# Nine-step Newton roots, layer-norm roots in the heads' chain, and three more tiles turned early

## The chip, the cores and the metric

The kernel runs on one core of one Trainium2 chip. The metric is the time of one execution on the device in microseconds (us). The time to compare with is the median of several runs of the same kernel; one further execution is taken with the hardware profiler, and all rows below are from that one.

## The reference, cut to what matters

The input x is 4 x 512 rows of 512 values. Two layers are added to it.

```
x = x + attn(layernorm(x))            # 16 heads of 32, linear attention with decay, chunks of 128
    q, k = rotate(silu(xn @ Wq)), rotate(silu(xn @ Wk));  v = xn @ Wv
    per chunk: scores = (q k^T) * D;  o = scores v + (q * decay_q) S;  S = lam S + (k * decay_k)^T v
    o = rmsnorm_per_head(o * sigmoid(xn @ Wg1 @ Wg2)) * norm_weight;  return o @ Wo
x = x + ffn(layernorm(x))             # weights in 4-bit codes with a scale per 32
    gelu(x @ Wg^T) * (x @ Wu^T) @ Wd^T      with MLP_DIM = 4096
```

Both the layer norm (one root for each row of x) and the norm of the gated heads (16 roots for each row) need a reciprocal square root.

## The kernel before, in words

Everything is written out by hand: each engine has its own program, in order, and the engines meet at semaphores. There is no scheduler; the order of the lines of an engine's program is the order of its work.

**Attention.** The 2048 rows are 16 tiles of 128 (`t = 4 * b + c`, batch b, chunk c). Tiles 0 to 13 are the body `tile(b, c)` of each engine, 14 and 15 are written out in `passage()`, interleaved with the first products and transposes of the second layer (`x1`, `x1_sums`, `gate`, `up`). In one tile TensorE does in order: `qk_transpose(t)` (line 1256, from `qr`); `k_project(t+1)` (12 matmuls); `gate1(t+1)`; `v_project(t+1)` (12); the scores (line 1341); `x_transpose(t+2)`; `o_part(t-1)` (12, the output projection of the tile before); `inter` (not in chunk 0) and `intra`; the state product (not in chunk 3); `q_part(t+2)` (12) with `o_back(t)` (line 1381) in its midst; `gate2(t+1)`. Products of 32-bit data are three matmuls of high and low parts (lines 1242 to 1244).

`o_transpose(t-1)` (line 1256, from `sq`) stands before `v_project` where t is in `TURNED_EARLY`, and after it elsewhere. Where t is in `TURNED_EARLY`, `gate1(t+1)` is also done `together`: four matmuls over 256 columns (line 1307), high and low parts side by side, which VectorE then adds (`sum_gate`); elsewhere it is eight over 128 columns (lines 1303, 1304). In tile 14 `o_transpose` stands before `v_project` too.

**VectorE** (DVE) does in one tile: `normed(t-1)`: wait for ScalarE's square, a sum per head (line 733), the root of 16 values a row by Newton's method (`newton`, lines 651 to 658, eleven steps, each waiting for the one before), and the multiplication that makes `sq` (line 737); `decayed_q(t)` (`qdT`, line 839); gate, rotation (`rope_of`, line 803) and low parts in an order that depends on `TURNED_EARLY`; `masked(t)`, four operations on the scores (line 845); `add_x1(t-1)` with the statistics of the finished row; then, in some tiles, more; then `gated(t)` (line 727), which needs `o_back(t)`; and the state. What "more" is: `stats_r(8, 16, 3)` in tile 4 and `stats2(0)`, `stats2(1)` in tiles 11 and 13 are the layer norm's roots, with a Newton chain of their own; `unit_bits` in tiles 5, 7, 9 (five operations, lines 760 to 771, which unpack 4-bit codes in `stg`) and `unit_scale` in tiles 6, 8, 10 (line 777).

After `gated(t)` ScalarE (ACT) squares `xg`, and `normed(t)` of the next tile can go on. GpSimd (POOL) does the second half of the rotation (lines 1096, 1104), the decayed keys, the sums and low parts of the unpacked weights, and from tile 12 on `x1_sums(n)`, eight groups for the second layer, each four scalings and four sums.

**Second layer.** 32 `pair`s in a loop (`blocks`), 14 products a pair and the rows of the pair before, with VectorE and ScalarE in their shade.

Of the kernel before, what the change touches and what calls it, by code (L numbers as in the profile page):

```python
# [52 lines left out]
TURNED_EARLY = (2, 3, 4, 6, 7, 9, 11, 12)  # L53
# [28 lines left out]
def build(nc, x, wq, wk, wv, wo, wg1, wg2, norm_w, packed, scales,  # L82
          rot, mask, decay_q, decay_k, lam_c, ident, out):
    ctx = ExitStack()
    with ctx:
# [20 lines left out]
        nt_v = sb("nt_v", [P, 16])  # L106
        nt_t = sb("nt_t", [P, 16])
# [11 lines left out]
        with ExitStack() as att:  # L119
# [30 lines left out]
            rr = sb("rr", [P, HEADS], F32, att)  # L150
# [74 lines left out]
        st_scaled, st_done = sem("st_scaled"), sem("st_done")  # L225
        xg_done, sq_done, ms_done, on_done = (sem("xg_done"), sem("sq_done"), sem("ms_done"),
# [16 lines left out]
        NT = 11  # L243
# [394 lines left out]
        def _(dve):  # L638
            V = nc.vector

            def newton(steps, v, n, r, base, scale, eps):

                vv, tt = nt_v[:, 0:n], nt_t[:, 0:n]
# [7 lines left out]
                done(V.tensor_scalar(vv, v, scale, eps, ALU.mult, ALU.add))  # L651
# [78 lines left out]
            def normed(t):  # L730
# [5 lines left out]
                newton(s_nt, ms[:], HEADS, rr[:], NT * t, 1.0 / HD, 4 * RMS_EPS)  # L736
                V.tensor_tensor(sq[:].rearrange("p (h d) -> p h d", d=HD),
                                xg[:].rearrange("p (h d) -> p h d", d=HD),
                                rr[:].unsqueeze(2).broadcast_to([P, HEADS, HD]),
# [16 lines left out]
            def unit_bits(k):  # L756
# [13 lines left out]
                dve.wait_ge(dq_bits, k5 + 4)  # L770
# [12 lines left out]
            def stats2(n):  # L783
# [7 lines left out]
                newton(s_ntl, ln2[:, rows, 1], last - first, r2[:, rows], NT * (4 + n), 1.0,  # L791
# [231 lines left out]
            def pair(q, p):  # L1023
# [19 lines left out]
                if p == 1 and ready:  # L1043
                    unit_bits(UNITS + GATE)
# [721 lines left out]
```

## Time and profile before

| what | value |
|---|---|
| median of 3 runs | 1284.52 us (1284.4 to 1286.33) |
| the profiled execution, its own time | 1285.71 us |
| its span, first to last instruction | 1283.5 us |
| TensorE busy | 1268.5 us, 99% |
| VectorE busy | 915.4 us, 71% |
| ScalarE, GpSimd busy | 476.7 us, 439.7 us |
| mean granted clock of TensorE | 0.999 |

In the rows below a time is in microseconds from the span's start. PE is TensorE, DVE VectorE, ACT ScalarE, POOL GpSimd. Matmuls are pipelined: the duration of one reaches into the next, so the cost of a matmul is read from one start to the next. The idle time in brackets is the engine's time without work before that row, and behind the arrow stands what ended it. The attention stage lasts to about 315 us, with the passage from about 273 to 340; the rest is the loop.

### The profile page before, as it was taken

The page shows a single profiled execution, that of the slowest core. Times are in us where ns is not written, and L with a number is a line of the kernel's source. Part 1 is how long each engine was busy: PE and PEld are TensorE (multiplying, and loading weights), DVE is VectorE, ACT ScalarE, POOL GpSimd, SP SyncE. Part 2 cuts the span into 40 slices and gives each one's busy share as a digit, 9 for nine tenths or more (in the row PEclk, how much of TensorE's full clock was granted, in tenths as well). Part 3 has the DMA queues.
Part 4 walks back from the last instruction along what each step waited for, and adds up shares of the span by engine and source line. Part 5 has one row for each costly group of instructions (what it writes and reads, how often), then busy time and mean ns, then how long its engine had stood idle before and what let it go on. Part 6 is the DMA issues. An engine that isn't in the chain of part 4 may idle for free.

```text
span 1283.5 us, 20667 instructions
## 1 busy us (share of the span) xinstructions
PE 1268.5 (99%) x7344; PEld 1042.4 (81%) x7344; DVE 915.4 (71%) x1602; ACT 476.7 (37%) x807; POOL 439.7 (34%) x360
## 2 busy tenths in 40 slices
PE   9999999999999999999999999999999999999998
PEld 6888877887788888888888888888888888888887
DVE  7888788788867667676667676766767676767565
ACT  5433443434433333333333333333333333333321
POOL 2434553674432232324132423233232324232400
PEclk9999999999999999999999999999999999999999
DMA  9000000000001011000000000100001010000003
GB/s 324 13 1 3 17 17 2 2 1 2 28 22 33 16 33 32 17 33 32 25 25 25 25 31 18 33 16 33 25 25 33 25 33 25 25 25 25 25 14 118
DMA packets 21778, 40.23 MB, mean 31 GB/s; under 512 B 2660, under 2 KB 2916, under 8 KB 21604
## 3 DMA queue, kind: packets, MB, share of 16 engines
q1 hardware_dynamic: 21060, 39.47, 9.5%
q8 instruction: 31, 0.51, 0.2%
q10 hardware_dynamic: 672, 0.13, 0.1%
q14 instruction: 15, 0.12, 0.0%
HBM read 35.40 MB, written 4.19 MB: 31 GB/s over the span
## 4 chain that ended last, share of the span: by engine, by line
PE 90%; DVE 6%; POOL 1%; issue 1%; ACT 0%; DVEq 0%; POOLq 0%
PE bank L1401 15%; PE bank L1403 15%; PE bank L1404 15%; PE bank L1242 12%; PE bank L1244 12%; PE bank L1243 12%; PE bank L1256 2%; PE bank L1341 1%; PE bank L1360 1%; DVE pr L845 1%; PE bank L1393 1%; PE bank L1350 1%; DVE nt_t L657 1%; PE bank L1381 0%; POOL ws L1178 0%
## 5 line engine op out<-in xcount | busy, mean ns | idle before, releaser
L926 DVE TENSOR_TENSOR acc<-acc,bank 128x512 f32<-128x512 f32 x248 | 169.6, 684 | 134.8 <-PE bank L1244 134.8
L1243 PE MATMUL bank<-wdl,hh 128*128 128x512 f32 x512 | 199.2, 389 | 0.0
L1242 PE MATMUL bank<-wdh,hh 128*128 128x512 f32 x512 | 199.2, 389 | 0.0
L1244 PE MATMUL bank<-wdh,hl 128*128 128x512 f32 x512 | 199.2, 389 | 0.0
L1401 PE MATMUL bank<-xoh,wuh 128*128 128x512 f32 x448 | 175.1, 391 | 0.7 <-ACT cxa L506 0.7
L1401 PE MATMUL bank<-xoh,wgh 128*128 128x512 f32 x448 | 175.1, 391 | 0.6 <-DVE cxa L934 0.6
L1404 PE MATMUL bank<-xoh,wul 128*128 128x512 f32 x448 | 174.4, 389 | 0.0
L1404 PE MATMUL bank<-xoh,wgl 128*128 128x512 f32 x448 | 174.3, 389 | 0.0
L1403 PE MATMUL bank<-xol,wuh 128*128 128x512 f32 x448 | 174.3, 389 | 0.0
L1403 PE MATMUL bank<-xol,wgh 128*128 128x512 f32 x448 | 174.3, 389 | 0.0
L1150 POOL TENSOR_TENSOR wdl<-ws,wdh 128x512 fp32r<-128x512 f32 x32 | 48.5, 1539 | 307.5 <-ACT wdh L432 307.5
L942 DVE TENSOR_TENSOR hl<-hx,hh 128x512 fp32r<-128x512 f32 x128 | 104.8, 819 | 51.4 <-ACT hh L513 51.1
L513 ACT ACTIVATE hh<-hx 128x512 fp32r<-128x512 f32 x128 | 80.6, 631 | 157.1 <-DVE hx L938 156.9
L506 ACT ACTIVATE cxa<-bank 128x512 f32<-128x512 f32 x64 | 38.3, 598 | 215.9 <-PE bank L1404 215.9
L1242 PEld LDWEIGHTS bank<-wdh,hh 128*128 128x128 f32 x512 | 96.1, 188 | 20.0
L1244 PEld LDWEIGHTS bank<-wdh,hl 128*128 128x128 f32 x512 | 96.1, 188 | 20.0
L1243 PEld LDWEIGHTS bank<-wdl,hh 128*128 128x128 f32 x512 | 96.1, 188 | 19.9
L1143 POOL TENSOR_TENSOR wul<-ws,wuh 128x896 fp32r<-128x896 f32 x32 | 74.2, 2339 | 84.6 <-ACT wuh L428 84.6
L1401 PEld LDWEIGHTS bank<-xoh,wuh 128*128 128x128 f32 x448 | 84.1, 188 | 18.6 <-ACT cxa L506 1.4
L1401 PEld LDWEIGHTS bank<-xoh,wgh 128*128 128x128 f32 x448 | 84.1, 188 | 18.6 <-DVE cxa L934 1.0
L1404 PEld LDWEIGHTS bank<-xoh,wgl 128*128 128x128 f32 x448 | 84.1, 188 | 17.5
L1404 PEld LDWEIGHTS bank<-xoh,wul 128*128 128x128 f32 x448 | 84.1, 188 | 17.5
(170 smaller groups left out, 2280.9 us busy)
## 6 DMA issues: line engine op xcount, KB each, us to landing
stg<-packed_dram SPq DMA_DIRECT2D x48, 256.0 KB, 2.6
stg<-scales_dram SPq DMA_DIRECT2D x48, 256.0 KB
out_dram<-acc SPq DMA_DIRECT2D x16, 256.0 KB, 2.1
acc<-x_dram SPq DMA_DIRECT2D x3, 1024.0 KB, 14.8
w_in<-wq_dram SPq DMA_DIRECT2D x2, 512.0 KB, 5.3
w_in<-wk_dram SPq DMA_DIRECT2D x2, 512.0 KB, 7.2
w_in<-wv_dram SPq DMA_DIRECT2D x2, 512.0 KB, 8.9
w_in<-wo_dram SPq DMA_DIRECT2D x2, 512.0 KB, 11.5
```

The costliest lines, as they stand in the source:

```text
L506: A(dst, src[:], ACT.Copy).then_inc(signal, 1)
L513: A(hh[n][:], hx[n][:], ACT.Copy).then_inc(h_hi[n], 1)
L926: V.tensor_tensor(row, row, BY[j % 2][:], ALU.add).then_inc(y_add, 1)
L942: V.tensor_tensor(hl[n][:], hx[n][:], hh[n][:].bitcast(F32), ALU.subtract).then_inc(h_lo[n], 1)
L1143: nc.gpsimd.tensor_tensor(lo[:, piece, :, :], ws[:, piece, :, :], hi[:, piece, :, :].bitcast(F32), ALU.subtract).then_inc(dq_lo, 1)
L1150: nc.gpsimd.tensor_tensor(wdl[:, piece, :].rearrange("p (s m) -> p s m", s=4), ws[:, piece, 0:4, :], wdh[:, piece, :].bitcast(F32) .rearra ...
L1242: pe.matmul(dst, w_h, x_h, start=start, stop=False)
L1243: pe.matmul(dst, w_h, x_l, start=False, stop=False)
L1244: return pe.matmul(dst, w_l, x_h, start=False, stop=stop)
L1401: pe.matmul(dst[:], w_h, x_h, start=start and a == 0, stop=False, skip_group_check=True)
L1403: pe.matmul(dst[:], w_h, x_l, start=False, stop=False, skip_group_check=True)
L1404: ins = pe.matmul(dst[:], w_l, x_h, start=False, stop=a == 1, skip_group_check=True)
```

## The change

It has these parts.

- `TURNED_EARLY` has 5, 8 and 10 in addition.
- `newton` takes nine steps in place of eleven, for all its callers: two refinements of another form in place of three.
- The layer norm's roots of rows 8 to 15 (tile 4), of the second norm's rows 0 to 7 (tile 11) and 8 to 12 (tile 13) are no longer made in those tiles. `normed_and_rows` makes them in tiles 5, 12 and 14, in the chain that makes the heads' roots there: the aggregates and `var_of` before, up to 24 values in the chain, `roots_out` after.
- The bits of units 1 and 2 (tiles 7 and 9) and the scaling of them (tiles 8 and 10) stand right after `normed(t-1)`; the last of the five operations of `unit_bits` is now `unit_join`, and is done right before the scaling there.
- GpSimd's `x1_sums(2)` stands first in `passage()`, ahead of the last tile's rotation.
- In `pair`, `low_of(C22, ...)` stands ahead of the first `total`.

```diff
-TURNED_EARLY = (2, 3, 4, 6, 7, 9, 11, 12)
+TURNED_EARLY = (2, 3, 4, 5, 6, 7, 8, 9, 10, 11, 12)
...
-        NT = 11
+        NT = 9
...
-                for _ in range(3):
-                    done(V.scalar_tensor_tensor(out=tt, in0=r, scalar=-0.5, in1=r,
-                                                op0=ALU.mult, op1=ALU.mult))
-                    done(V.tensor_tensor(tt, tt, vv, ALU.mult))
-                    done(V.scalar_tensor_tensor(out=r, in0=tt, scalar=1.5, in1=r,
-                                                op0=ALU.add, op1=ALU.mult))
+                done(V.tensor_tensor(tt, r, r, ALU.mult))
+                done(V.tensor_tensor(tt, tt, vv, ALU.mult))
+                done(V.scalar_tensor_tensor(out=tt, in0=tt, scalar=-10.0 / 3.0, in1=tt,
+                                            op0=ALU.add, op1=ALU.mult))
+                done(V.scalar_tensor_tensor(out=r, in0=tt, scalar=5.0, in1=r,
+                                            op0=ALU.add, op1=ALU.mult))
+                done(V.scalar_tensor_tensor(out=tt, in0=r, scalar=-27.0 / 1024.0, in1=r,
+                                            op0=ALU.mult, op1=ALU.mult))
+                done(V.tensor_tensor(tt, tt, vv, ALU.mult))
+                done(V.scalar_tensor_tensor(out=r, in0=tt, scalar=9.0 / 16.0, in1=r,
+                                            op0=ALU.add, op1=ALU.mult))
...
+            def var_of(ln, first, last):
+
+                V.tensor_scalar(nt_v[:, HEADS:HEADS + last - first], ln[:, first:last, 1], 1.0,
+                                LN_EPS, ALU.mult, ALU.add).then_inc(var_in, 1)
+
+            def roots_out(ln, r, nm, first, last, k, signal, n):
+                rows, new = slice(first, last), rr[:, HEADS:HEADS + last - first]
+                V.scalar_tensor_tensor(out=nm[:, rows], in0=ln[:, rows, 0], scalar=-1.0, in1=new,
+                                       op0=ALU.mult, op1=ALU.mult).then_inc(nm_out, 1)
+                dve.wait_ge(nm_out, k + 1)
+                V.tensor_copy(r[:, rows], new).then_inc(signal, n)
+
+            def normed_and_rows(t, ln, r, nm, first, last, k, signal, n):
+                for row in range(first, last):
+                    if signal is s_r1:
+                        dve.wait_ge(s_bn1, row + 1)
+                        V.bn_aggr(ln[:, row, :], bst1[:, row, :]).then_inc(s_ln1, 1)
+                    else:
+                        dve.wait_ge(bst_done, row + 1)
+                        V.bn_aggr(ln[:, row, :], bst1[:, row, :]).then_inc(ln2_done, 1)
+                dve.wait_ge(s_ln1 if signal is s_r1 else ln2_done, last)
+                var_of(ln, first, last)
+                dve.wait_ge(var_in, k + 1)
+                normed(t, last - first)
+                roots_out(ln, r, nm, first, last, k, signal, n)
...
-                dve.wait_ge(dq_bits, k5 + 4)
+
+            def unit_join(k):
+                dve.wait_ge(dq_bits, 5 * k + 4)
                 V.tensor_tensor(nib, nib, pk, ALU.bitwise_or).then_inc(dq_bits, 1)
...
-                if not at_start(b, c):
+                if t == 5:
+                    normed_and_rows(4, ln1, r1, nm1, 8, 16, 0, s_r1, 2)
+                elif t == 12:
+                    normed_and_rows(11, ln2, r2, nm2, 0, 8, 1, s_r2, 1)
+                elif not at_start(b, c):
                     normed(t - 1)
+                if t in UNIT_BITS[1:]:
+                    unit_bits(UNIT_BITS.index(t))
+                if t in UNIT_SCALE[1:]:
+                    unit_join(UNIT_SCALE.index(t))
+                    unit_scale(UNIT_SCALE.index(t))
                 decayed_q(t)
...
-                if t == 4:
-                    stats_r(8, 16, 3)
-                if t == 11:
-                    stats2(0)
-                if t == 13:
-                    stats2(1)
-                if t in UNIT_BITS:
-                    unit_bits(UNIT_BITS.index(t))
-                if t in UNIT_SCALE:
-                    unit_scale(UNIT_SCALE.index(t))
+                if t == UNIT_BITS[GATE]:
+                    unit_bits(GATE)
+                    unit_join(GATE)
+                if t == UNIT_SCALE[GATE]:
+                    unit_scale(GATE)
                 gated(t)
...
-                normed(s - 1)
+                normed_and_rows(s - 1, ln2, r2, nm2, 8, 13, 2, s_r2, 1)
...
+                low_of(C22, P_ - 1)
                 dve.wait_ge(g_ps, 7 * P_ + 2)
                 dve.wait_ge(g_copy, 3 * P_ + 1)
                 total(GB[:], GB, hx[C11][:], g_sum)
-                low_of(C22, P_ - 1)
                 up_12(P_ - 1)
...
             def passage():
+                x1_sums(2)
                 rope_b_(TILES - 1, CHUNKS - 1)
                 scaled(BATCH - 1, CHUNKS - 2)
-                for n in range(2, 8):
+                for n in range(3, 8):
                     x1_sums(n)
```

## Rows read from the trace of the kernel before

**Rows 1.** The page, busy time of each engine

```profile
PE 1268.5 (99%) x7344; PEld 1042.4 (81%) x7344; DVE 915.4 (71%) x1602; ACT 476.7 (37%) x807; POOL 439.7 (34%) x360
```

**Rows 2.** TensorE's timeline, the first instructions of tiles 4 to 11: start, duration

```profile
92.99 1.03 PE L1256 MATMUL bank<-idt,qr 128*128 128x128 f32 x8
...
109.68 1.04 PE L1256 MATMUL bank<-idt,qr 128*128 128x128 f32 x8
...
127.92 1.03 PE L1256 MATMUL bank<-idt,qr 128*128 128x128 f32 x8
...
145.72 1.04 PE L1256 MATMUL bank<-idt,qr 128*128 128x128 f32 x8
...
163.13 1.04 PE L1256 MATMUL bank<-idt,qr 128*128 128x128 f32 x8
...
182.26 1.03 PE L1256 MATMUL bank<-idt,qr 128*128 128x128 f32 x8
...
199.95 1.03 PE L1256 MATMUL bank<-idt,qr 128*128 128x128 f32 x8
...
220.38 1.03 PE L1256 MATMUL bank<-idt,qr 128*128 128x128 f32 x8
```

**Rows 3.** TensorE's timeline, the gate's first part in tile 7 and tile 8

```profile
149.35 0.64 PE L1307 MATMUL bank<-xt,g1s 128*128 128x256 f32 x4
149.82 0.60 PE L1256 MATMUL bank<-idt,sq 128*128 128x128 f32 x4
...
166.76 0.22 PE L1303 MATMUL bank<-xt,g1s 128*128 128x128 f32 x1
...
167.60 0.45 PE L1242 MATMUL bank<-w_hi,xt 128*128 128x512 f32 x1
```

**Rows 4.** VectorE's timeline, from the gated product of tile 6 to `sq`

```profile
143.60 0.69 DVE L727 SCALAR_TENSOR_TENSOR xg<-tg,bank 128x512 f32<-128x512 f32 x1 [1.04 <-PE bank L1381]
...
145.71 0.18 DVE L651 TENSOR_SCALAR nt_v<-ms 128x16 f32<-128x16 f32 x1
...
148.01 0.69 DVE L737 TENSOR_TENSOR sq<-xg,rr 128x512 f32<-128x512 f32 x1
```

**Rows 5.** TensorE's timeline, `o_back` of tile 7

```profile
161.07 0.60 PE L1381 MATMUL bank<-idt,xg 128*128 128x128 f32 x4
```

**Rows 6.** VectorE's timeline, from the gated product of tile 7 to `sq`

```profile
164.31 0.68 DVE L727 SCALAR_TENSOR_TENSOR xg<-tg,bank 128x512 f32<-128x512 f32 x1
...
168.30 1.20 DVE L657 TENSOR_TENSOR nt_t<-nt_t,nt_v 128x16 f32<-128x16 f32 x1
...
170.78 0.69 DVE L737 TENSOR_TENSOR sq<-xg,rr 128x512 f32<-128x512 f32 x1
```

**Rows 7.** VectorE's groups by line: busy us, mean ns, idle before

```profile
L777 DVE SCALAR_TENSOR_TENSOR ws<-stg 128x1024 f32<-128x1024 f16 x48 | 58.5, 1219 | 0.0
...
L763 DVE SCALAR_TENSOR_TENSOR stg<-stg 128x512 int32<-128x512 int32 x48 | 35.8, 745 | 1.6
```

**Rows 8.** TensorE's timeline, idle before `sq`'s transposes in tile 12 and the passage

```profile
242.50 0.66 PE L1256 MATMUL bank<-idt,sq 128*128 128x128 f32 x4 [0.46 <-DVE sq L737]
...
278.82 0.66 PE L1256 MATMUL bank<-idt,sq 128*128 128x128 f32 x4 [0.84 <-DVE sq L737]
...
294.46 0.65 PE L1256 MATMUL bank<-idt,sq 128*128 128x128 f32 x4 [1.15 <-DVE sq L737]
```

**Rows 9.** VectorE's timeline, the Newton chain in tile 13

```profile
255.14 0.17 DVE L651 TENSOR_SCALAR nt_v<-ms 128x16 f32<-128x16 f32 x1
...
259.25 0.69 DVE L737 TENSOR_TENSOR sq<-xg,rr 128x512 f32<-128x512 f32 x1
```

**Rows 10.** ScalarE's timeline at the start of the kernel

```profile
8.60 0.81 ACT L359 ACTIVATE xn<-acc,nm,r 128x512 f32<-128x512 f32 x1 [1.20 <-DVE nm L675]
```

**Rows 11.** GpSimd's timeline, its rotation for tile 15

```profile
278.33 2.85 POOL L1096 TENSOR_TENSOR rb<-qa,rotT 128x512 f32<-128x512 f32 x2 [2.01 <-ACT qa L397]
```

**Rows 12.** Windows: busy us and instructions by engine, granted clock, DMA share, GB/s

```profile
298.00:300.00 2.00, 2.00 (x11) 2.00 (x10) 0.64 (x2) 1.38 (x4) 0.23 (x1) 0.50 0.00 0
```

More of the change, by code:

```diff
@@ L105, in build @@
         nm2 = sb("nm2", [P, TILES])
-        nt_v = sb("nt_v", [P, 16])
-        nt_t = sb("nt_t", [P, 16])
+        nt_v = sb("nt_v", [P, 24])
+        nt_t = sb("nt_t", [P, 24])
         bst1 = sb("bst1", [P, TILES, 6])
@@ L639, in _, with newton @@
             V = nc.vector
-            def newton(steps, v, n, r, base, scale, eps):
-                vv, tt = nt_v[:, 0:n], nt_t[:, 0:n]
+            def newton(steps, v, n, r, base, scale, eps, more=0):
+                vv, tt = nt_v[:, 0:n + more], nt_t[:, 0:n + more]
                 k = [0]
@@ L649, in done @@
                     dve.wait_ge(steps, base + k[0])
-                done(V.tensor_scalar(vv, v, scale, eps, ALU.mult, ALU.add))
+                done(V.tensor_scalar(nt_v[:, 0:n], v, scale, eps, ALU.mult, ALU.add))
                 done(V.tensor_scalar(r.bitcast(I32), vv.bitcast(I32), -0.5, RSQRT_SEED,
                                      ALU.mult, ALU.add))
-                for _ in range(3):
-                    done(V.scalar_tensor_tensor(out=tt, in0=r, scalar=-0.5, in1=r,
-                                                op0=ALU.mult, op1=ALU.mult))
-                    done(V.tensor_tensor(tt, tt, vv, ALU.mult))
-                    done(V.scalar_tensor_tensor(out=r, in0=tt, scalar=1.5, in1=r,
-                                                op0=ALU.add, op1=ALU.mult))
+                done(V.tensor_tensor(tt, r, r, ALU.mult))
[9 more added lines that the diff above has]
+                                            op0=ALU.add, op1=ALU.mult))
                 assert k[0] == NT
@@ L728, in gated, with normed @@
                                        op0=ALU.add, op1=ALU.mult).then_inc(xg_done, 1)
-            def normed(t):
+            def var_of(ln, first, last):
[20 more added lines that the diff above has]
+                roots_out(ln, r, nm, first, last, k, signal, n)
+            def normed(t, more=0):
                 dve.wait_ge(sq_done, t + 1)
@@ L735, in normed @@
                 dve.wait_ge(ms_done, t + 1)
-                newton(s_nt, ms[:], HEADS, rr[:], NT * t, 1.0 / HD, 4 * RMS_EPS)
+                newton(s_nt, ms[:], HEADS, rr[:, 0:HEADS + more], NT * t, 1.0 / HD, 4 * RMS_EPS, more)
                 V.tensor_tensor(sq[:].rearrange("p (h d) -> p h d", d=HD),
                                 xg[:].rearrange("p (h d) -> p h d", d=HD),
-                                rr[:].unsqueeze(2).broadcast_to([P, HEADS, HD]),
+                                rr[:, 0:HEADS].unsqueeze(2).broadcast_to([P, HEADS, HD]),
                                 ALU.mult).then_inc(on_done, 1)
@@ L790, in stats2 @@
                 dve.wait_ge(ln2_done, last)
-                newton(s_ntl, ln2[:, rows, 1], last - first, r2[:, rows], NT * (4 + n), 1.0,
+                newton(s_ntl, ln2[:, rows, 1], last - first, r2[:, rows], NT * (1 + n), 1.0,
                        LN_EPS)
@@ L1044, in pair @@
                     unit_bits(UNITS + GATE)
+                    unit_join(UNITS + GATE)
                 if p == 1 and not last:
@@ L1056, in pair @@
                     unit_bits(3 * q + DOWN)
+                    unit_join(3 * q + DOWN)
                 y(4)
@@ L1068, in pair @@
                     unit_bits(3 * q + 3 + UP)
+                    unit_join(3 * q + 3 + UP)
                 y(6)
@@ L1071, in pair @@
                     unit_bits(3 * q + 3 + GATE)
+                    unit_join(3 * q + 3 + GATE)
                 if p == 1 and not last:
```

3 lines of the change are left out of this document (2 added, 1 removed).

## The prediction

> **What bounds the kernel now.** I read the page first: TensorE is busy for 99% of the span [rows 1], so only two things can save time, fewer TensorE microseconds or fewer gaps between them. The second view is TensorE's own timeline in the attention stage. A tile begins with the eight transposes of the rotated q and k (line 1256, out of `qr`). From one such row to the next is a tile's length [rows 2]: tile 4 takes 109.68 - 92.99 = 16.69 us, tile 5 18.24, tile 6 17.80, tile 7 17.41, tile 8 19.13, tile 9 17.69 and tile 10 20.43. Tiles 4, 6, 7 and 9 are turned early, tiles 5, 8 and 10 are not. A tile's work depends on its chunk: chunk 0 has no `inter`, chunk 3 no state product. So tile 8 (chunk 0) is to be compared with tile 4, tile 5 (chunk 1) with tile 9, and tile 10 (chunk 2) with tile 6. The third view is VectorE's timeline, for what TensorE waits for at `o_transpose`: the normed heads `sq`.
>
> VectorE's clean chain is that of tile 6 into 7 [rows 4]: the gated product starts at 143.60, as soon as `o_back` is there, and the multiplication that ends `normed` at 148.01, so 4.41 us plus about 0.7 for the multiplication, 5.1 in all. Eleven Newton steps fill 145.71 to 148.01, 0.21 us each. Early TensorE comes to `o_transpose` at 149.82, which is 4.10 after the tile's start at 145.72 [rows 2, 3], and finds `sq` done since 148.7. Tile 7 into 8 is the unclean chain. `o_back` starts at 161.07 and takes 0.6 [rows 5], yet the gated product starts only at 164.31, because `unit_bits(1)` stands ahead of it in VectorE's queue, and then two Newton steps show 1.20 us or so in place of 0.17 [rows 6], in which GpSimd holds what they need. The multiplication starts at 170.78 and TensorE has long run dry. Tile 10 repeats this with `unit_bits(2)`.
>
> **The change, part by part.**
>
> *Turned early, 5, 8 and 10.* The first part of the gate takes four matmuls of 256 columns in place of eight of 128: 149.82 - 149.35 = 0.47 us against 167.60 - 166.76 = 0.84 [rows 3]. That is 0.37 a tile. The trace's 128-column matmuls therefore cost 0.105 apiece and the 256-column ones 0.118. The Trainium skill (TensorE: Matmul & The Clock Gate, Back-to-back issue gap) makes the gap proportional to columns above an issue floor, about 56 ns at 128 and twice that at 256. By it the merging would save nothing and the sum below would be 1.1 us smaller; the trace disagrees, with 0.84 against 0.47, and I go by the trace. The rest of what an early tile saves is smoother order, and is in the tile lengths. Tile 5 has no long wait now, so it goes from 18.24 to tile 9's 17.69: **0.55 us**.
>
> *Tiles 8 and 10.* Early order asks for `sq` at 4.10 after the tile's start, 167.23 in tile 8's present times, though it is done only at 171.5 now. What makes it earlier: `unit_bits` of tiles 7 and 9 moves ahead of `decayed_q`, so the gated product starts at 161.07 + 0.63 = 161.70, not 164.31 (2.6 us); the chain falls 2.6 earlier, before GpSimd's rotation starts on q, so the two long steps become short (2.05 us); and there are nine steps in place of eleven (0.42). 161.70 + 5.1 - 0.42 = 166.4, with 0.8 to spare. So the tiles should reach the clean lengths: tile 8 19.13 - 16.69 = **2.44 us**, tile 10 20.43 - 17.80 = **2.63 us**. Bounds: nothing gained at all, when the chain is late by 2.5 and more, and those two numbers.
>
> *What the moved work meets.* Ahead of `decayed_q`, tiles 8 and 10 now have the join and the scaling, about 0.7 and 1.22 us [rows 7], and tiles 7 and 9 the bits, some 2.1 us by the 0.745 of the costliest of four [rows 7]. TensorE needs `qdT` and the gate's sum before the scores, 7.4 us after the start. 3.3 (end of `sq`) + 1.9 + 0.7 + 0.3 = 6.2, covered by 1.2 us. Masking then starts perhaps 0.3 late, since the rotation on VectorE may have to let GpSimd finish; after it TensorE still has the scores, the transposes of x and `o_part`, so this costs nothing. Without that cover each of the four tiles would lose up to 1.9 us. The rule behind it is that of the Trainium skill (SBUF — State Buffer, SBUF: two separate sides): VectorE operations with two SBUF inputs and GpSimd's exclude each other for a whole instruction. The 1.20 us steps [rows 6] agree with it, and it would forbid moving two-input work into GpSimd's time; the join, the rotation and the Newton steps are such work.
>
> *The shared chains.* In tile 4 `stats_r(8,16)` delays the gated product, in tile 11 `stats2(0)` and in tile 13 `stats2(1)`. Now rows join the chain of the heads: what stays of each are the aggregates (some 0.6 for eight), one scaling before, a product and a copy after, 0.2 each. Aggregates and scaling lie beside ScalarE's square, which VectorE waits for anyway (0.5), and push the chain by 0.2 to 0.5; the product and the copy come after `sq`. TensorE's stalls at those places are 0.46 idle in tile 12 and 0.84 in tile 14 [rows 8], to which the pipeline's drain adds about 0.15 (in tile 8 0.94 idle is 1.09 from start to start). In tile 12 I take all of it, **0.6**. In tile 14 the chain will meet GpSimd's second x group as that of tile 13 meets the first: there eleven steps took 255.14 to 259.25, 4.11 in place of 2.3 [rows 9]. By that row `sq` ends 4.5 after the start, with TensorE there at 4.46. I take **0.7** of 1.0, between 0 and 1.0.
>
> *Two steps fewer elsewhere.* At the start of the kernel ScalarE waits 1.20 us for VectorE's first root [rows 10] and TensorE's first projection hangs on it: two steps of 0.2, **0.4 us** (0 if a load or ScalarE's casts come last). At 294.46 TensorE sits idle for 1.15 behind `sq` of tile 14 [rows 8]; two steps and about 0.4 of slowing by GpSimd, whose third group no longer lies there, give **0.8** (0.4 to 1.3). For the last two groups of rows, the end of the transposes and the first pair, where VectorE is again last, I allow **0.4** (0 to 1.2).
>
> *GpSimd's third group* goes into its idle 2.01 us ahead of the rotation for tile 15 at 278.33 [rows 11], and is longer than that (the four x scalings and four sums), so that rotation comes some microseconds later; TensorE transposes what it makes only after the stall at 294.46 [rows 8], 14 us on. Cost 0.
>
> *The pair loop.* `low_of(C22)` goes ahead of the first total. TensorE shows no gap in the loop's 30 pairs that VectorE could close or open: 0. The joins there only follow their bits: 0.
>
> **Sum.** 0.55 + 2.44 + 2.63 + 0.6 + 0.7 + 0.4 + 0.8 + 0.4 = 8.5 us. The profiled execution took 1285.71 (span 1283.5), which would be 1277.2; it lies 1.2 above the median of the runs, 1284.52, and against that, which is what the new time is compared with, the forecast is 1276.0.
>
> **Rivals.**
>
> 1. *The clock stays up.* Between 298 and 300 the granted clock is 0.50 [rows 12], 1.2 GHz, after the gap ahead of 294.46 [rows 8]. Where the clock is at 0.50 matmul work takes twice as long, so 3 us at it cost 1.5. Shorter gaps there may keep it at 2.4 GHz and give that back: 1274.5. Against it: by my own count some of the gap remains. The Trainium skill (TensorE: Matmul & The Clock Gate, The HAM clock gate) says that recent activity keeps the gate open, which allows this but doesn't decide it.
>
> 2. *GpSimd still holds the chain.* In tiles 8 and 10 two steps are lengthened as now, 2.05 us [rows 6]: `sq` ends 5.3 after the start, not 3.3, TensorE waits 1.2 in each, and 0.5 is lost behind tile 5, whose bits still stand ahead of the gated product: 1276.0 + 2.9 = 1278.9. For it: GpSimd's sums after a scaling now start at another time. Against it: its rotation waits for ScalarE's q, which comes after the chain.
>
> 3. *The other side: early order asks for what is still late.* If the gated product of tiles 7 and 9 is not freed, `sq` of tile 8 ends at 171.5, and early TensorE stands from 167.2: 4.2 of waiting in place of the 2.44 and 2.63 lost now. With the bits' and the scaling's 1.9 us each before `qdT` on top, which have no cover then, that is 1.8 + 1.6 + 3.8 = 7.2 more than now, less the other 3.4: 1288.3. It decides against the change from about 5.5 us of lateness in each of the two tiles on. Against it: `o_back` is done 2.6 before the gated product starts [rows 5, 6], and nothing but the bits lies between.
>
> 4. *The gaps only move.* What tiles 8 and 10 gain is given back where VectorE is nearly full, in tiles 9, 11 and the passage, because everything comes earlier for TensorE but not for VectorE: within 0.2% of 1284.5.
>
> **How the numbers follow.** Forecast 0.66, the clock 0.12, GpSimd 0.14, gaps that move 0.05, the other side 0.03. A difference of 0.2%, 2.6 us, is about what can be told from no change. Faster are the first three, 0.92; same 0.05; slower 0.03. The range goes from the clock's case with all bounds good, 1273.2, to the GpSimd case with its smaller terms lost, 1280.6.
>
> **What would show it.** Tile lengths near 17.7 for tile 5, 16.7 for 8 and 17.8 for 10; the gated product 0.6 after `o_back` starts in tiles 7, 9, 11 and 13; no idle of TensorE before the transposes of `sq` in tiles 8, 10 and 12; nine steps in each chain; GpSimd's third group ahead of the last rotation. The prediction is wrong if the transposes of `sq` in tiles 8 and 10 have idle time of more than a microsecond ahead of them, if scores wait for `qdT`, or if the passage between 273 and 340 grows.

## The result, and the profile after

The changed kernel takes 1277.34 us in the median of 4 runs (1275.86 to 1278.02), the kernel before in the same set 1284.91 (1284.4 to 1286.33). The ratio is 0.994, with a 95% interval of 0.9925 to 0.9954: faster by 0.5 to 0.75%. The forecast was 1276.0. In a second set of 5 runs the same changed kernel took 1276.63, ratio 0.9938 (0.9925 to 0.9952), against 1284.50 for the kernel before in that set. The profiled execution has a span of 1276.0 (before 1283.5); its own time is 1278.02, the longest of its set.

The head of the page after, to be read against [rows 1]:

```profile
span 1276.0 us, 20589 instructions
PE 1264.7 (99%) x7332; PEld 1040.4 (82%) x7332; DVE 897.2 (70%) x1535; ACT 479.1 (38%) x810; POOL 439.9 (34%) x360
```

VectorE has 18 us less to do. TensorE is busy for 3.8 us less and idle for 3.7 less (15.0 before, 11.3 after), so the gain lies half in its work and half in its gaps. TensorE's timeline, the first transposes of each tile from 4 to 13, against [rows 2]:

```profile
92.34 1.03 PE L1299 MATMUL bank<-idt,qr 128*128 128x128 f32 x8
109.02 1.04 PE L1299 MATMUL bank<-idt,qr 128*128 128x128 f32 x8
126.73 1.04 PE L1299 MATMUL bank<-idt,qr 128*128 128x128 f32 x8
144.44 1.04 PE L1299 MATMUL bank<-idt,qr 128*128 128x128 f32 x8
161.85 1.03 PE L1299 MATMUL bank<-idt,qr 128*128 128x128 f32 x8
178.54 1.03 PE L1299 MATMUL bank<-idt,qr 128*128 128x128 f32 x8
196.24 1.04 PE L1299 MATMUL bank<-idt,qr 128*128 128x128 f32 x8
213.95 1.03 PE L1299 MATMUL bank<-idt,qr 128*128 128x128 f32 x8
231.36 1.03 PE L1299 MATMUL bank<-idt,qr 128*128 128x128 f32 x8
248.05 1.04 PE L1299 MATMUL bank<-idt,qr 128*128 128x128 f32 x8
```

From start to start: tile 4 16.68, tile 5 17.71, tile 6 17.71, tile 8 16.69, tile 10 17.71, tile 12 16.69. From tile 4 to 12 every tile of one chunk number now has one length. Tile 13 (chunk 1), which is not turned early, takes 18.21 as tile 5 did before. In tile 8 the gate's product takes 0.47 from start to start, as [rows 3] had it for an early tile, and the transposes of `sq` have no idle time ahead of them:

```profile
165.46 0.63 PE L1350 MATMUL bank<-xt,g1s 128*128 128x256 f32 x4
165.93 0.60 PE L1299 MATMUL bank<-idt,sq 128*128 128x128 f32 x4
```

VectorE's timeline from tile 7 into 8, against [rows 4, 6]:

```profile
160.43 0.69 DVE L733 SCALAR_TENSOR_TENSOR xg<-tg,bank 128x512 f32<-128x512 f32 x1 [2.15 <-PE bank L1424]
161.81 0.69 DVE L765 TENSOR_REDUCE ms<-sq 128x16 f32<-128x512 f32 x1 [0.70 <-ACT sq L419]
162.53 0.17 DVE L652 TENSOR_SCALAR nt_v<-ms 128x16 f32<-128x16 f32 x1
...
164.21 0.18 DVE L664 SCALAR_TENSOR_TENSOR rr<-nt_t,rr 128x16 f32<-128x16 f32 x1
164.42 0.69 DVE L769 TENSOR_TENSOR sq<-xg,rr 128x512 f32<-128x512 f32 x1
165.03 0.68 DVE L805 TENSOR_TENSOR stg<-stg 128x512 int32<-128x512 int32 x1
165.75 1.22 DVE L811 SCALAR_TENSOR_TENSOR ws<-stg 128x1024 f32<-128x1024 f16 x1
166.89 0.68 DVE L873 TENSOR_TENSOR qdT<-bank,dqT 128x512 f32<-128x512 f32 x1
```

VectorE now idles 2.15 us in wait of `o_back` where it was late before, the nine steps are 0.21 apart, and `sq` is done at 165.1, 0.8 before TensorE asks for it. The join and the scaling stand behind it, as planned, and `qdT` is there 1.6 before the scores, which start at 169.22.

The idle places of the passage, TensorE's timeline, against [rows 8]; the last one, at 320.96, has its counterpart in one of 0.24 at 328.02 in the kernel before:

```profile
271.18 0.66 PE L1299 MATMUL bank<-idt,sq 128*128 128x128 f32 x4 [0.30 <-DVE sq L769]
286.29 0.66 PE L1299 MATMUL bank<-idt,sq 128*128 128x128 f32 x4 [0.60 <-DVE sq L769]
...
320.96 0.41 PE L1436 MATMUL bank<-idt,ws 128*128 128x128 f32 x2 [1.17 <-POOL stg L1228]
```

And the stretches of the passage in which the clock fell, against [rows 12] (engines' busy time, then the granted clock, the DMA share and GB/s):

```profile
288.00:290.00 2.00, 1.37 (x7) 1.40 (x8) 2.00 (x6) 0.98 (x3) 1.92 (x4) 0.65 0.02 4
290.00:292.00 2.00, 2.00 (x11) 2.00 (x10) 0.47 (x1) 1.38 (x4) 0.62 (x1) 0.50 0.00 0
```

The granted clock was 0.50 (1.2 GHz) for 3.4 us, from 288.6 to 292.0, as it was from 297.0 to 300.4 in the kernel before. So none of the 7.5 us is the clock's.

**Where the time came from.** The lead of after over before, read at the same instruction in both traces: 0.44 at the first tiles, 7.09 at tile 14's start, 8.17 at the transposes of `sq` at 286.29, 8.02 at the first product of the second layer (298.76), 7.06 at 320.96, 7.55 at the last pair, 7.5 at the end. So 8.2 were gained by 286, which is more than the kernel has at the end: about 1 us is lost again in one place, between 298.76 and 320.96.

What is late there is VectorE. Its timeline, the last row's root chain of the kernel before and of the one after:

```profile
324.01 0.17 DVE L789 BATCH_NORM_AGGREGATE ln<-bst 128x2 f32<-128x6 f32 x1
324.59 0.28 DVE L655 SCALAR_TENSOR_TENSOR nt_t<-r 128x1 f32<-128x1 f32 x1
...
327.19 0.69 DVE L870 TENSOR_TENSOR xol<-bank,xoh 128x512 fp32r<-128x512 f32 x1
```

```profile
316.00 0.17 DVE L823 BATCH_NORM_AGGREGATE ln<-bst 128x2 f32<-128x6 f32 x1
316.59 0.42 DVE L655 TENSOR_TENSOR nt_t<-r 128x1 f32<-128x1 f32 x1
...
317.62 0.57 DVE L659 SCALAR_TENSOR_TENSOR r<-nt_t,r 128x1 f32<-128x1 f32 x1
...
319.56 0.65 DVE L827 SCALAR_TENSOR_TENSOR nm<-ln,r 128x1 f32<-128x1 f32 x1
320.13 0.68 DVE L904 TENSOR_TENSOR xol<-bank,xoh 128x512 fp32r<-128x512 f32 x1
```

With eleven steps it took 3.18 us from the aggregate to the next low part; with nine it takes 4.13. The low part `xol` frees the bank that TensorE's transposes at 320.96 write; the row's label names GpSimd's `stg`, but these transposes read `ws`, whose last sum had ended at 316.44; that `stg` belongs to the next group. GpSimd works beside the chain all the time, on the seventh group of sums:

```profile
316.42 2.27 POOL L1220 TENSOR_SCALAR stg<-acc,r,nm 128x256 f32<-128x256 f32 x4
```

### The profile page after: what moved, and what is told of

Its sections match the earlier page's. It is cut to its first block, busy times and chain, and to the rows that moved or that the text cites. A ratio compares the mean times of both kernels' runs of the same rounds, so it can differ in the third digit from the quotient of the medians.

```text
span 1276.0 us, 20589 instructions
## 1 busy us (share of the span) xinstructions
PE 1264.7 (99%) x7332; PEld 1040.4 (82%) x7332; DVE 897.2 (70%) x1535; ACT 479.1 (38%) x810; POOL 439.9 (34%) x360
## 4 chain that ended last, share of the span: by engine, by line
PE 94%; DVE 2%; POOL 1%; issue 0%; ACT 0%; POOLq 0%; DVEq 0%
PE bank L1444 16%; PE bank L1446 16%; PE bank L1447 15%; PE bank L1285 13%; PE bank L1287 13%; PE bank L1286 13%; PE bank L1299 2%; PE bank L1384 1%; PE bank L1403 1%; PE bank L1393 1%; PE bank L1436 1%; PE bank L1424 1%; DVE xol L904 0%; PE bank L1350 0%; PE bank L1416 0%
## 5 line engine op out<-in xcount | busy, mean ns | idle before, releaser
L980 DVE TENSOR_TENSOR hl<-hx,hh 128x512 fp32r<-128x512 f32 x128 | 101.7, 795 | 52.1 <-ACT hh L514 51.6
```

What stands on the lines that cost most here:

```text
L980: V.tensor_tensor(hl[n][:], hx[n][:], hh[n][:].bitcast(F32), ALU.subtract).then_inc(h_lo[n], 1)
```

## The experiments

Twelve runs follow: eleven edits and the changed kernel once more. They ran in three sets, in which the kernel before took 1284.71 (`a`, `b`, `c`, `e`), 1285.54 (`d`, `f`, `g`, `h`) and 1284.50 (`after_again`, `j`, `m`, `n`); between sets the ratios are to be compared, not the medians. "Lengths" are tile lengths as above. "The passage" is split at three rows that every trace has: tile 14's start, the first product of the second layer (the gate's), and the gate's product of the first pair that waits for `cxa` (343.92 in after). In the tables, "chain" is from the last row's aggregate to VectorE's next operation on 128 x 512.

### Early order, the moved units, the shared chains

`a_no_early`: the early list as before, all else changed. `b_early_only`: the kernel before with the new list alone. `c_units_late`: the units' bits, join and scaling back ahead of `gated`. `e_own_chains`: the layer norm's rows in chains of their own.

```diff
 a:  TURNED_EARLY = (2, 3, 4, 6, 7, 9, 11, 12)          # in the changed kernel
 b:  TURNED_EARLY = (2, 3, 4, 5, 6, 7, 8, 9, 10, 11, 12) # in the kernel before
 c: -if t in UNIT_BITS[1:]: ...   -if t in UNIT_SCALE[1:]: ...
    +if t in UNIT_BITS: unit_bits(...); unit_join(...)     # ahead of gated(t)
    +if t in UNIT_SCALE: unit_scale(...)
 e: -normed_and_rows(...)  in tiles 5, 12, 14
    +normed(t - 1);  stats_r(8, 16, 3), stats2(0), stats2(1) in tiles 4, 11, 13
```

> The changed kernel with the old list of tiles turned early (5, 8 and 10 not). Theory one, the freed chain: nearly all of the gain is that VectorE delivers sq in time, and the early order is worth some 0.5 us a tile; tiles 5, 8 and 10 become 18.2, 17.2 and 18.2 us, TensorE has no wait for sq there, and the time is 1277.3 + 1.5 = 1278.8. Theory two, the order: the gain comes with the early order and goes with it; tiles 8 and 10 go back to about 19.1 and 20.4, and the time is about 1282.9.

> The kernel before with 5, 8 and 10 turned early and nothing else. The freed chain: in tiles 8 and 10 TensorE comes to the transposes of sq 4.2 us before sq is there; tiles of some 20.9 and 22 us, tile 5 between 17.7 and 18.3, in all 2 to 3.5 us slower than before, about 1287.6. The order: tiles 5, 8 and 10 near 17.7, 16.7 and 17.8, about 1279.3.

> The changed kernel with the bits and scalings of units 1 and 2 back at the end of their tiles, ahead of the gated product. The freed chain: sq of tiles 7 and 9 is late again by 2.6 us and meets GpSimd's rotation, TensorE waits 3 to 4 us before its transposes in tiles 8 and 10, 7 us in all: 1284.3. The order, or the shorter chains, being the cause: no change, 1277.3.

> The changed kernel with the layer norm's roots back in chains of their own at the end of tiles 4, 11 and 13. If the shared chain is what freed tiles 5, 12 and 14: waits of TensorE for sq of about 0.6, 0.3 and 0.8 us there, 1.4 us slower than the changed kernel, 1278.7. If nine steps and the rest do it without the sharing: no such waits, 1277.3.

| kernel | median, ratio (95%) | span | tile 5 | tile 8 | tile 10 | tile 12 |
|---|---|---|---|---|---|---|
| before | 1284.91 | 1283.5 | 18.24 | 19.13 | 20.43 | 17.38 |
| after | 1277.34, 0.994 (0.9925, 0.9954) | 1276.0 | 17.71 | 16.69 | 17.71 | 16.69 |
| a_no_early | 1277.81, 0.9944 (0.9928, 0.9961) | 1275.8 | 18.20 | 17.14 | 18.22 | 16.68 |
| b_early_only | 1294.78, 1.0084 (1.0067, 1.0101) | 1291.1 | 18.80 | 22.56 | 23.88 | 17.37 |
| c_units_late | 1283.4, 0.9995 (0.9985, 1.0004) | 1280.2 | 17.71 | 19.55 | 20.84 | 16.69 |
| e_own_chains | 1277.66, 0.9948 (0.9932, 0.9965) | 1275.6 | 17.98 | 16.69 | 17.70 | 16.67 |

`a_no_early` gave the lengths of its first theory. The early order alone makes the kernel slower, by 10 us in the medians and by 7.6 in the span of the profiled executions, of which 7.4 lie in tiles 5, 8 and 10; I had expected 2 to 3.5. With the other parts it is worth 0.49 + 0.45 + 0.51 = 1.45 us by the lengths; the ratios of after and `a_no_early`, 0.994 and 0.9944, don't tell the two apart. TensorE's timeline of `b_early_only` shows what it asks for too early:

```profile
172.03 1.12 PE L1256 MATMUL bank<-idt,sq 128*128 128x128 f32 x4 [4.10 <-DVE sq L737]
212.52 0.71 PE L1256 MATMUL bank<-idt,sq 128*128 128x128 f32 x4 [4.37 <-DVE sq L737]
```

That is rival 3's 4.2, in the kernel where its condition holds. What I had left out is the clock: behind each of the two waits it fell to 1.2 GHz for 3.4 us, which costs half of that (windows, columns as above).

```profile
172.00:174.00 2.00, 1.98 (x7) 1.79 (x8) 0.96 (x3) 0.80 (x2) 0.00 (x0) 0.51 0.03 8
213.00:215.00 2.00, 2.00 (x7) 1.62 (x6) 1.36 (x4) 1.21 (x3) 0.00 (x0) 0.50 0.04 8
```

The clean length, the wait and 1.7 for the clock make up the tiles: 16.7 + 4.1 + 1.7 = 22.5 for tile 8 (22.56), 17.8 + 4.4 + 1.7 = 23.9 for tile 10 (23.88). With the chains shortened but the units left in place, in `c_units_late`, there is still 2.7 and 2.9 of waiting at the same two places:

```profile
168.98 0.66 PE L1294 MATMUL bank<-idt,sq 128*128 128x128 f32 x4 [2.67 <-DVE sq L769]
206.50 0.66 PE L1294 MATMUL bank<-idt,sq 128*128 128x128 f32 x4 [2.93 <-DVE sq L769]
```

So the move of two small groups of VectorE instructions carries 2.86 + 3.13 = 6.0 us under the early order, and with the units in their old place the kernel is no faster than before (0.9995). In the profiled execution of `c_units_late` the clock did not fall in these tiles; four of its ten runs took 1285.0 to 1286.6 at a mean clock of 0.996 or 0.997, the other six 1282.3 to 1283.4 at 0.999 or 1.0. Without the early order it and the shorter chain still give 1.99 + 2.21 (`a_no_early` against before). The parts don't add up one by one: early order is minus 7.4 without the move, about 3.4 of it the clock's, and plus 1.45 with it.

The shared chains are worth less than I had them. In `e_own_chains` tile 12 is as short as in after, and so it is in `d_eleven_steps` below (16.67), which shares the chain and keeps eleven steps: either part alone gives the 0.69. What taking the sharing away costs is 0.27 in tile 5 and 0.56 in tile 14, where the idle time before `sq` is 0.85 instead of 0.30. That makes 0.8 us by the trace; the ratios (0.9948 and 0.994) don't tell it from nothing.

### The nine steps

`d_eleven_steps`: the changed kernel with three Newton steps, eleven instructions, as in before.

```diff
-NT = 9     +NT = 11
-two refinements, seven steps     +for _ in range(3): ... three steps each
```

> The changed kernel with the root chain of eleven steps (three Newton steps) of before in place of the nine. By the sum: the chains in tiles 5 to 13 are off the path that sets the end, so their tiles keep their lengths (16.7 to 17.7); 0.4 comes back at the start (39.0 to 39.4), 0.3 to 0.4 in tile 14 or at the idle of 0.60 before scores(15), 0.3 at x1(23): together about 1.0, 1278.3 (1277.9 to 1278.8). A rival, that the chains still set the gate in tiles 8 and 10: 0.4 more for each, 1279.1 or above. Another, that the one row's chain has nothing to do with 320.96: 1277.9 and the idle there stays at 1.17.

It took 1279.19 (0.9951; 0.9934 to 0.9967), span 1276.7. Tiles 8, 10 and 12 keep their lengths, as expected; tile 2 is 0.26 longer (17.92 against 17.66) and tile 6 0.11. The idle time before `sq` is 0.91 in tile 14 and 1.16 behind it, where `after_again` has 0.28 and 0.62: with the rest of the passage up to the first gate product that is 32.46 us against 31.29, 1.17 for the two steps. In tile 14 nine steps alone (`e_own_chains`, 0.85) or the shared chain alone (0.91) leave an idle time like that of before, 0.84, both with GpSimd's third group at its early place; only both together take it down. The last row's chain takes 4.49 and the stall behind it 1.52 against 0.45. The sum is 0.26 + 0.11 + 1.17 + 1.10 = 2.6; the span is 2.4 above that of `after_again`, with a start 0.3 earlier. Of these the 1.10 can't be given to the steps alone, since that chain's length changes between executions, as the next section shows. Without it the two steps are worth 1.5, with it 2.6, and the ratios (0.9951 against 0.9938 in `after_again`) say 1.7, each with an interval of about 0.0015 either way. My expectation of about 1.0 was too low in any case.

### The place that gave 1 us back

`h_x21_first`: x1's group 21 before the last row's chain instead of behind it. `f_third_late`: GpSimd's third group back behind the rotation. `n_pool_waits`: GpSimd's seventh group waits for the last row's chain. `after_again`: the changed kernel itself.

```diff
 h: -x1(20, 20)                 +x1(20, 21)
     stats2(3)                   stats2(3)
    -x1(21, 21)
 f: -x1_sums(2)  ahead of rope_b_(TILES - 1, ...)   -range(3, 8)   +range(2, 8)
 n: -pool.wait_ge(s_r2, (1, 1, 1, 1, 2, 3, 3, 4)[i])
    +pool.wait_ge(s_r2, (1, 1, 1, 1, 2, 3, 4, 4)[i])
```

> The changed kernel, with the low part of x1 of row group 21 taken before the last rows' statistics and root chain instead of behind them. Theory one (the one row's chain, stretched by GpSimd's group beside it from 316.00 to 320.13, holds back the passage of group 21, so the bank that x1(23) writes is free 0.7 us later than it was against its neighbours): the idle of 1.17 us at 320.96 is gone or under 0.3, what the chain feeds is not asked for at once, and the time is 0.7 to 1.2 below the changed kernel's, about 1276.3. Theory two (the bank is not what is late, or GpSimd is): the idle stays near 1.2 and the time is the same, 1277.3 within 0.3. Theory three (the idle moves to the next gate or copy, where the r2 of the last rows is asked for): less than half of it comes back, 1277.0.

> The changed kernel, with GpSimd's sums of the third group of the second layer-norm back in their old place behind the rotation of the heads' scale. Theory one (that group lies beside VectorE's one-row chain and its steps are stretched from about 0.2 to 0.4 to 0.65 us): GpSimd's spans shift against the chain, the steps are nearer 0.2 to 0.3 each and the idle at 320.96 falls to 0.2 to 0.5, the time 0.3 to 0.9 lower than the changed kernel's if nothing else is late. My sum's own price for this part was 0, so 1277.3 within 0.3. A rival: the early place is what keeps the idle before scores(15) at 0.60; then that idle goes back to 1.15 and the time is 0.5 higher, 1277.9.

> The changed kernel once more, unaltered, beside the other three of this call. It tells what of the differences between profiled executions belongs to no edit. Theory one: the one row's chain (from 17.24 us behind the first gate product) is stretched by GpSimd by an amount that changes from execution to execution (3.2 to 4.6 us seen with the same distance between GpSimd's group and the chain), so this execution may show another chain and another stall than 3.9 and 1.17 us; the stall is the chain's excess over about 2.8. Theory two: it is fixed by the order, and the chain is 3.9 and the stall 1.17 again. Time 1277.3 within 1 in either case. TensorE's clock between the last tile's start and the first gate product either falls to half for about 2 us, as in the profiled execution, or not at all, as in six of the seven executions since.

> The changed kernel, with GpSimd's seventh of the eight groups of sums (the one that runs beside the last row's chain) made to wait for that chain. Theory one (the chain is stretched because GpSimd's operations run beside it): its nine steps take about 0.19 each, from the aggregate to nm 2.3 to 2.6 us instead of 3.9, and the stall of 1.17 before the gate product falls to under 0.3; GpSimd's seventh group starts some 2.2 later, so its transposes come late and 1 to 2 us are lost again one group further on; the time 1277.3 to 1278.8. Theory two (the chain is slow for a reason of its own, such as one row's operand): the steps keep their 0.4 to 0.65, the stall stays at 1.17, and GpSimd's delay comes on top, 4 us and more: 1279 to 1281.

| kernel | median, ratio (95%) | span | tile 14 to gate | gate to `cxa` | chain | stall behind it |
|---|---|---|---|---|---|---|
| before | | 1283.5 | 33.43 | 44.73 | 3.18 | 0.24 |
| after | 1277.34, 0.994 | 1276.0 | 32.50 | 45.16 | 4.13 | 1.17 |
| after_again | 1276.63, 0.9938 (0.9925, 0.9952) | 1274.3 | 31.29 | 44.44 | 3.41 | 0.45 |
| a_no_early | as above | 1275.8 | 31.31 | 44.47 | 3.45 | 0.49 |
| h_x21_first | 1277.67, 0.9938 (0.9922, 0.9955) | 1275.5 | 31.32 | 45.86 | 4.01 | 1.89 |
| f_third_late | 1276.83, 0.9937 (0.992, 0.9953) | 1274.3 | 31.11 | 45.16 | 4.12 | 1.16 |
| n_pool_waits | 1275.94, 0.993 (0.9915, 0.9945) | 1273.4 | 31.28 | 43.80 | 2.01 | none |

`n_pool_waits` settles what stretches the chain. VectorE's and GpSimd's timelines in it:

```profile
314.79 0.17 DVE L823 BATCH_NORM_AGGREGATE ln<-bst 128x2 f32<-128x6 f32 x1
315.37 0.16 DVE L655 TENSOR_TENSOR nt_t<-r 128x1 f32<-128x1 f32 x1
...
316.53 0.16 DVE L664 SCALAR_TENSOR_TENSOR r<-nt_t,r 128x1 f32<-128x1 f32 x1
...
316.80 0.68 DVE L904 TENSOR_TENSOR xol<-bank,xoh 128x512 fp32r<-128x512 f32 x1
```

```profile
317.09 2.23 POOL L1220 TENSOR_SCALAR stg<-acc,r,nm 128x256 f32<-128x256 f32 x4 [1.86 <-DVE nm L827]
```

Without GpSimd beside it every step takes 0.15 or 0.16, the chain 2.01 in place of 4.13 (or 3.41), and the stall is gone. My expectation missed that the delay of GpSimd, 1.86 us of idle, costs nothing further on: the next stall, 0.48 before the last transposes, is the 0.49 of the other kernels.

`after_again` is the same program as after, and its chain is 3.41 and its stall 0.45:

```profile
319.37 0.41 PE L1436 MATMUL bank<-idt,ws 128*128 128x128 f32 x2 [0.45 <-POOL stg L1226]
```

GpSimd's group starts 0.41 behind the aggregate in it, 0.42 in after. So the stretch is a matter of the execution, not of the order alone. Of the nine traces with nine steps and this order around the chain, in which GpSimd starts 0.40 to 0.43 behind the aggregate, six have a chain of 3.41 to 3.45 and a stall of 0.45 to 0.49, two 4.12 and 4.13, one 4.81. With eleven steps and GpSimd 0.82 behind the aggregate it was 3.18 in before, 3.14 in `b_early_only` and 4.49 in `d_eleven_steps`.

`h_x21_first` refutes my first reading. The low part went ahead, and the stall was not less but 1.89, one group of transposes further on: TensorE then waits for the low part behind the chain. VectorE had idled 1.14 for ScalarE's high part of group 21, so the chain began 1.8 later, 19.08 behind the first gate product in place of 17.24. The whole chain is what is late, and not one operation's place. TensorE's timeline:

```profile
322.18 0.63 PE L1435 MATMUL bank<-idt,stg 128*128 128x128 f32 x4 [1.89 <-POOL ws L1219]
```

`f_third_late` doesn't touch the stall at all (1.16), against what I expected; its chain of 4.12 is as long as after's. It shows another thing: the third group of sums at its early place runs beside the end of the chain that ends in tile 14, whose last steps are 0.28 and 0.20 in after and 0.18 in `f_third_late`. The idle time of 0.30 before `sq` in tile 14 is gone there, and tile 14 to the gate is 0.18 shorter than in `after_again`. The 0.60 one tile later stays. By these traces the early place costs 0.2 to 0.3 and brings nothing.

### Two more edits

`g_low_back`: `low_of(C22)` behind the first total again. `j_x7_first`: x1's group 7 ahead of `add_x1(s - 1)`. `m_f_and_j`: this and the third group late.

```diff
 g: -low_of(C22, P_ - 1)        j: -x1(6, 6)
     total(GB[:], ...)              +x1(6, 7)
    +low_of(C22, P_ - 1)             add_x1(s - 1)
                                   -x1(7, 7)
```

> The changed kernel with the low part of column block 22 split behind the products of the total instead of before them, as in before. By the sum this place is worth nothing: 1277.3 within 0.2. A rival: the first pair's total waits for the low part where it stood early, or the other way round, and 0.2 to 0.4 moves either way at the idle of 0.60 near 344.

> The changed kernel, with the low part of x1's group 7 taken before the last but one tile's add to the accumulator instead of behind it. Theory one (the idle of 1.02 us at 288.63, which both kernels have, is group 7's bank, held by VectorE's two operations of 0.67 and 0.69 ahead of its low part): the idle falls to about 0, and since the state and the next low parts keep their place, 0.5 to 1.0 comes back: 1276.5. Theory two (ScalarE's tg or the state is as late, so the idle only moves to the transposes of q and k behind it): within 0.3 of the changed kernel's.

> Both at once: the third group of sums late again and x1's group 7 first. The first alone took 1276.83 with a span of 1274.3, 1.7 below the changed kernel's. Theory one (each removes a wait of its own, 0.30 and about 0.8): 1275.9, ratio to before 0.993. Theory two (the differences between these orders are what the last row's chain and the clock happen to do in one execution): 1277 within 1, as all the others.

`g_low_back` took 1279.65 (0.9948; 0.9932 to 0.9965), 1277.88 to 1281.12 in its runs, span 1279.0. Two things of its profiled execution vary between executions of one program elsewhere: a chain of 4.81 with a stall of 1.85, and behind that stall a granted clock of 0.50 for 3.4 us, from 321.4 to 324.8. The third was not expected. From the first to the last `cxa` product the loop takes 916.20 us; in after it takes 914.94. TensorE's first gate products between 350 and 1250 us, `g_low_back` and then after:

```profile
L1444 PE MATMUL bank<-xoh,wgh 128*128 128x512 f32 x420 | 164.5, 392 | 0.0
```

```profile
L1444 PE MATMUL bank<-xoh,wgh 128*128 128x512 f32 x420 | 163.4, 389 | 0.0
```

In every second pair of `g_low_back`, 14 in all, one such product lasts 0.46 in place of 0.39 (the first at 400.26) and the next starts 0.07 late, which makes 1.0 of the 1.25; the rest I didn't find. `b_early_only`, the other late one with `low_of` in its old place, has 14 such products too and a loop of 916.15. The profiled execution of before has none, 914.90, and none of the 11 executions with `low_of` ahead has one. So the old place has two ways of running, 1.25 us apart, of which the trace that I argued from showed the good one. What chooses between them was not found. That the new place shuts out the bad one is likely by these counts, two of three against none of eleven, and not more than that.

`j_x7_first` took 1276.83 (0.9937; 0.9922 to 0.9952), span 1273.9. The idle time of 1.02 before group 7's transposes is gone, but tile 14 to the gate is 30.96, only 0.33 less than in `after_again`: 0.73 of idle time comes back before the transposes of q and k. That is theory two. `m_f_and_j` took 1275.99 (0.993; 0.9916 to 0.9943), span 1273.7, tile 14 to the gate 30.68: 0.61 less than in `after_again`, where the two alone take off 0.33 and 0.18. It and `n_pool_waits` are ahead of the changed kernel by 0.6 and 0.7 in the same set, inside the spread of single runs of the changed kernel (1275.86 to 1278.57 in both sets). I take both as likely gains by their traces, not by their times.

## Why the prediction was right, and where it was not

The kernel is faster, and mainly by the mechanism that was forecast: tiles 8 and 10, where the chain is freed, give 5.2 of the 7.5 us. The terms, by TensorE's timelines of before and after:

| term | forecast | measured | from |
|---|---|---|---|
| tile 5 | 0.55 | 0.53 | lengths |
| tile 8 | 2.44 | 2.44 | lengths |
| tile 10 | 2.63 | 2.72 | lengths |
| tile 12 | 0.6 | 0.69 | lengths |
| tile 14 | 0.7 | 0.54 | idle 0.84 to 0.30 |
| start | 0.4 | 0.44 | first tiles |
| behind tile 14 | 0.8 | 0.55 | idle 1.15 to 0.60 |
| later short chains | 0.4 (0 to 1.2) | -0.7 | lead 8.17 to 7.5 |
| not in the sum: tiles 2, 6 | 0 | 0.29 | 17.90 to 17.70, 17.80 to 17.71 |
| sum | 8.5 | 7.5 | spans |

**Tiles 8 and 10.** The gated product starts as soon as `o_back` is there, 2.6 earlier in its tile, and the two long steps are gone, as the second step of the sum had it. `c_units_late` confirms that it is the units' place. Rival 2, GpSimd holding the chain, didn't come true in these tiles. It did in tile 14, where the first three steps take 0.61 to 0.67. Rival 3 says that about 5.5 us of lateness in each tile decide against the change. By its own sums it is 8.5 / 2 = 4.2 us of waiting in each, and by `c_units_late` 2.7 and 2.9 were enough to bring the ratio back to 0.9995. The range has a small slip too: the bounds of the terms add up to 1272.9 and 1280.8, not 1273.2 and 1280.6.

**The term that failed** is the last of the sum. I allowed 0.4 for later chains, with 0 as the lower bound. It measured -0.7, because the last row's chain took 4.13 with nine steps and 3.18 with eleven, and 0.96 of the lead were lost behind it. That is bad luck of one execution in part: in `after_again` the chain takes 3.41, still 0.23 more than with eleven steps, and from the first gate product to `cxa` the kernel takes 44.44 in place of before's 44.73, a gain of 0.3 (44.4 to 44.5 in six of the nine traces of this order). So the size of 0.4 was about right for most executions, and a bound below nothing was missing. `n_pool_waits` shows what GpSimd takes: 2.1 us of the chain's 4.13, 1.4 of its 3.41. The Trainium skill (SBUF — State Buffer, SBUF: two separate sides) has the two engines exclude each other, for a whole instruction, where VectorE's has two SBUF inputs. The trace agrees in kind: steps of 0.16 become up to 0.65, and in tile 14 the first three steps of after end at 267.03, 267.72 and 268.42, each within 0.04 of the end of one of GpSimd's sums. But the first two of these have one input, which that clause does not cover, and the chain's length differs between executions at one distance.

**The shared chains.** I gave them 1.3 for tiles 12 and 14, which measured 0.69 and 0.54. In tile 12 the sharing or the two steps fewer would have done it alone; in tile 14 it took both. So the sizes came out right, but I had given to the sharing what is the steps' as much. It also gives 0.27 of tile 5's 0.53 (`e_own_chains`), where I had counted the early order alone.

**GpSimd's third group.** I let its move give a part of the 0.8 and cost 0. By `f_third_late` it gives nothing there (0.60 either way) and costs 0.2 to 0.3 in tile 14.

**The start** measured 0.44, but not all of it is the chain's. In after ScalarE's cast of the weights comes last, not VectorE's root (ScalarE's timeline, against [rows 10]):

```profile
7.19 1.06 ACT L344 ACTIVATE w_hi<-w_in 128x1024 fp32r<-128x1024 f32 x1 [3.16 <-DMA w_in<-wq_dram]
8.15 0.80 ACT L360 ACTIVATE xn<-acc,nm,r 128x512 f32<-128x512 f32 x1
```

It stands behind a load, which let it start at 7.19; in `after_again` it started at 7.81 and tile 0 at 25.42, later than in before (25.22). In five of the eleven traces with nine steps VectorE's root still comes last, by 0.17 to 0.86. Tile 0 starts at 24.79 to 25.68 with nine steps, in the median at 24.97, and at 25.11, 25.17 and 25.22 with eleven. So the two steps are worth about 0.2 here, and the rest of the 0.44 is the luck of one load.

**The pair loop** was priced at nothing; `g_low_back` says that the new place of `low_of(C22)` is probably worth 1.25 in some of the executions. The 1.25 is no part of the 7.5, since the trace of before had the good way of running.

**The clock.** Rival 1 did not happen in the profiled execution and happened in the second one, with the same gaps. 32.50 against 31.29 from tile 14 to the gate gives it a price of 1.2, where I had 1.5. The kernel before has such runs too: eight of its 13 in the set of `a_no_early` have a mean clock of 1.0 and took 1284.2 to 1285.3. So it isn't shown that the shorter gaps keep the clock up.

**The merging of the gate's products.** `a_no_early` measures the whole early order at 0.45 to 0.51 a tile, of which the rows' 0.37 is the merging. The Trainium skill (TensorE: Matmul & The Clock Gate, Back-to-back issue gap) gives the rule that I used, a gap proportional to the columns, for an isolated matmul; by it nothing would have come of that part. For a stream with weight loads the same section gives about 81 ns at 128 columns and 131 ns at 512, which grows more slowly than the columns. I had left that out. Neither fits these 32-bit products: 0.105 at 128 columns, 0.118 at 256 and 0.23 at 512. The eight products of the old form have eight weight loads, 0.11 from start to start, the four of the new one have four; whether the loads set the pace was not tested.

## What to carry to other kernels

When an instruction is to be asked for earlier, first find what stands ahead of its producer in that engine's queue: here the early order cost 7.4 us before two groups of VectorE work were moved, and gave 1.45 after. A chain of tiny dependent steps that shares its time with GpSimd has no fixed length; let GpSimd wait for it where GpSimd has slack, and give such a chain a bound below nothing when its steps are cut. And run the same program twice before a microsecond is given to an edit: chain, clock and first load each moved the time by 0.6 to 1.2 us between executions of one program.

## What was not expected of the hardware

- Steps on one value per partition, 128 x 1, take 0.15 to 0.16 us alone and 0.16 to 0.66 beside GpSimd's scalings of 128 x 256. With GpSimd starting 0.40 to 0.43 behind the aggregate, the chain took 3.41 to 3.45 us in six traces, 4.12 and 4.13 in two and 4.81 in one; what chooses between them was not found.
- TensorE's clock fell to 1.2 GHz for 3.4 us in the passage in the profiled executions of before, of after and, at another place, of `g_low_back`, and in the passage of none of the eleven others (`b_early_only` has falls behind its idle times of 4.1 and 4.4 in tiles 8 and 10). `after_again` has the same idle times of 0.62 and 1.02 us ahead of the place as after (0.60 and 1.02), `b_early_only` those of before (1.15 and 1.02). So the length of these gaps didn't decide it here.
- The pair loop with one order of instructions ran at 914.9 or at 916.2 us, by whether one product in each second pair was 0.07 late.
